# Ending a feed-forward stage on the issue of its last stores, and moving a small scale computation one step earlier

## The reference

```python
xn = _layernorm(x)
x = x + attention(xn) + ffn(xn)          # ffn: gelu, weights reduced to alpha * sign
xn = _layernorm(x)
x = x + time_mix(xn) + experts(xn)       # time_mix: a scan over time
                                         # experts: router, 2 of 8 experts, and shared ones
```

## Time and profile before

| | us |
|---|---|
| median of 3 runs | 1522.09 (1521.3 to 1522.88) |
| the profiled execution | 1525.42 |
| its span, first to last instruction | 1523.3 |
| PE / DVE / ACT / POOL busy in the span | 1321.9 / 1288.7 / 987.5 / 320.6 |
| feed-forward, start and end in the span | about 921 to 1114 |
| time-mix, start and end in the span | about 1114 to 1307 |

### The profile page before, as it was taken

One profiled execution on the slowest core, in us unless ns is written; L12 is line 12 of the kernel. 1 busy time (PEld: TensorE's weight loads), 2 busy tenths in 40 slices (PEclk: granted clock), 3 DMA queues, 4 the chain that ended last, 5 costly groups with the idle time before them and its releaser, 6 DMA issues. The chain is left out here.

```text
span 1523.3 us, 27407 instructions
## 1 busy us (share of the span) xinstructions
PE 1321.9 (87%) x9558; PEld 600.1 (39%) x9558; DVE 1288.7 (85%) x2289; ACT 987.5 (65%) x1292; POOL 320.6 (21%) x574
## 2 busy tenths in 40 slices
PE   4776999999999999999999987999667767799886
PEld 2444223232232332223233213766434334477654
DVE  6886899999999999999999914899769999755667
ACT  3452365888888888888888895666266554356541
POOL 3220000111102011020111113333000177200655
PEclk9987688999999999999999998999878879899999
DMA  6886402140424204242241025785354155776756
GB/s 207 272 262 200 63 26 45 27 85 16 82 45 67 59 6 78 45 82 45 33 88 40 11 48 160 200 279 165 140 156 144 53 174 188 230 241 208 219 174 224
DMA packets 158520, 186.15 MB, mean 122 GB/s; under 512 B 18228, under 2 KB 134708, under 8 KB 157364
## 3 DMA queue, kind: packets, MB, share of 16 engines
q1 hardware_dynamic: 135384, 151.45, 37.1%
q0 software_dynamic: 6144, 16.79, 3.4%
q10 hardware_dynamic: 16864, 16.26, 3.1%
HBM read 100.81 MB, written 83.36 MB: 121 GB/s over the span
## 5 line engine op out<-in xcount | busy, mean ns | idle before, releaser
L1324 DVE TENSOR_REDUCE att_m_part<-att_mx 128x1 f32<-128x512 f32 (+3 forms) x1152 | 680.4, 653 | 30.4 <-PE att_mx L1392 13.6
L1354 ACT ACTIVATE att_prob<-att_score,late_score_scale 128x1024 f32<-128x1024 f32 (+3 forms) x640 | 595.3, 987 | 166.1 <-PE att_score L1431 164.1
L1392 PE MATMUL att_mx<-early_kop,early_qop 48*128 48x512 f16 (+3 forms) x1280 | 354.9, 367 | 23.3 <-DVE att_neg_m L1303 6.3
L1414 PE MATMUL att_pv<-att_prob,early_v 128*32 128x512 f32 (+3 forms) x2560 | 304.1, 547 | 2.1 <-POOL att_prob L1291 2.0
L1431 PE MATMUL att_score<-early_qop,early_kop 50*128 50x512 f16 (+3 forms) x1280 | 252.9, 356 | 11.2 <-ACT att_prob L1354 10.1
L1392 PEld LDWEIGHTS att_mx<-early_kop,early_qop 48*128 48x128 f16 x1280 | 98.5, 94 | 374.3 <-DVE att_m_part L1324 346.2
L1291 POOL TENSOR_SCALAR_AFFINE_SELECT att_prob<-att_prob 128x256 f32<-128x256 f32 x256 | 103.0, 408 | 669.6 <-ACT att_prob L1354 668.8
L2193 PE MATMUL rwkv_prod<-rwkv_xm,late_mixT 128*128 128x512 f32 x192 | 99.9, 676 | 33.3 <-ACT rwkv_kvr L2147 20.2
L1431 PEld LDWEIGHTS att_score<-early_qop,early_kop 50*128 50x128 f16 x1280 | 72.1, 94 | 72.0 <-ACT att_prob L1354 56.0
L2411 POOL DMA_INDIRECT moe_yg<-results,routing_slot_i x64 | 64.1, 1002 | 133.0 <-PE moe_turn_ps L2638 102.8
L1956 POOL DMA_INDIRECT rows<-rwkv_xs,routing_slot_i x64 | 66.5, 1040 | 115.3 <-DVE routing_slot_i L2047 96.1
(11 more groups left out here) (261 smaller groups left out, 1764.6 us busy)
## 6 DMA issues: line engine op xcount, KB each, us to landing
va<-qkv_v SPq DMA_DIRECT2D x8, 1024.0 KB, 6.3
early_v<-va SPq DMA_DIRECT2D x8, 1024.0 KB, 7.3
routing_xp<-parts SPq DMA_DIRECT2D x32, 256.0 KB, 3.6
moe_xt<-rows SPq DMA_DIRECT2D x30, 256.0 KB, 3.6
rows<-att_zeros SPq DMA_DIRECT2D x8, 864.0 KB, 6.2
early_kop<-qk SPq DMA_DIRECT2D x48, 128.0 KB, 4.5
results<-moe_y ACTq DMA_DIRECT2D x24, 256.0 KB, 2.6
results<-blend_x ACTq DMA_DIRECT2D x22, 256.0 KB, 2.7
```

The lines of the kernel that those rows point to most:

```text
L1324: nc.vector.tensor_reduce(cells[:, sides[0]:sides[-1] + 1, some], mx[:, banks[0]:banks[-1] + 1, 0:len(hps) * w].rearrange("p a (h w) -> p ...
L1354: nc.scalar.activation(prob[:, r % (PROBS * HP), :, n0:], score[:, r % 2, :, n0:], ACT.Exp, scale=late_weights.score_scale[:, 0:1])\
L1392: op = nc.tensor.matmul(bank[:, n * w:(n + 1) * w], qop[rows, slot, t, hp, i * P:(i + 1) * P], kop[rows, slot, hp, c * GT:c * GT + w], sta ...
L1414: op = nc.tensor.matmul(pv[at, n0:], v[:, slot, j, at], prob[:, (st * HP + h // 2) % (PROBS * HP), h % 2, n0:], start=(j == 0), stop=(j == ...
```

## The change

Four edits.

1. The feed-forward's SP stream no longer waits for the landing of its stores. The six semaphores that count them move to `BlendInputs`, which both phases hold. The time-mix's SP stream begins with the six waits and then raises a new semaphore, `landed`. DVE waits for `landed` in the time-mix before the router's `below_top` and before the first `outcome`.
2. The two loads of the time-mix's first inputs move one round of `body` earlier on SP: they stand after `body(G - 1)` instead of after `body(G)`, five stores earlier.
3. The expert scales move ahead of the last group's low part on DVE. On PE the turn of the maxima stands ahead of the last `ln.turn` and the spread behind it.
4. The scales use a bank of `hid_ps` instead of one of `out_ps`.

```diff
@@ PowerScale
     def tensor(self, nc, pe, turn, spread, ident, ones):
+        self.tensor_turn(nc, pe, turn, ident)
+        self.tensor_spread(nc, pe, spread, ones)
...
@@ ffn_phase, SP
             for g in range(G - 2, G + 2):
                 body((g, g % 2, 0), False, g - 1 < G, True)
-                if g == G:
+                if g == G - 1:
                     sp.wait_ge(zero_stored, 16 * B)
                     sp.wait_ge(xn_out[0], 48 * (1 + T // GT // 2 + 1))
                     for b in range(B):
                         blended.load(sp, xn1T_d, b)
-            for slot in range(2):
-                sp.wait_ge(x1_out[slot], 16 * (1 + G // 2))
-                sp.wait_ge(rows_out[slot], 16 * (1 + G // 2))
-                sp.wait_ge(xn_out[slot], 48 * (1 + G // 2))
@@ ffn_phase, DVE
                 if old:
                     output(*old)
+                if older and older[0] == G - 1:
+                    expert_weights.vector(nc, dve, hid_ps[:, 0, 0:C])
+                    expert_weights.router_parts(nc, dve)
                 if older:
...
             unrolled(step, 4)
-            expert_weights.vector(nc, dve, out_ps[:, 0])
-            expert_weights.router_parts(nc, dve)
@@ ffn_phase, PE
                     if old and tile == 3:
+                        if not mid:
+                            pe.wait_ge(gelu_done.sem, gelu_done.done(G * FC - 1))
+                            expert_weights.tensor_turn(nc, pe, hid_ps[:, 0, 0:C])
                         ln.turn(nc, pe, old[0], old[1], ident[:, :])
+                        if not mid:
+                            expert_weights.tensor_spread(nc, pe, hid_ps[:, 0, 0:C])
...
             rolling(pe, step, 3)
-            pe.wait_ge(x1_done.sem, x1_done.done(G - 1))
-            expert_weights.tensor(nc, pe, out_ps[:, 0])
@@ BlendInputs
+        self.x1_out = [s.sem(f"x1_out{p}") for p in range(2)]
+        self.xn_out = [s.sem(f"xn_out{p}") for p in range(2)]
+        self.rows_out = [s.sem(f"rows_out{p}") for p in range(2)]
+        self.landed = s.sem("landed")
+
+    def wait_landed(self, eng):
+
+        for slot in range(2):
+            eng.wait_ge(self.x1_out[slot], 16 * (1 + G // 2))
+            eng.wait_ge(self.rows_out[slot], 16 * (1 + G // 2))
+            eng.wait_ge(self.xn_out[slot], 48 * (1 + G // 2))
+        eng.sem_inc(self.landed, 1)
@@ rwkv_phase, SP
+            blended.wait_landed(sp)
             for dst, src in ((consts, route_d), (count.rearrange("p two t -> p (two t)"), count_d)):
@@ rwkv_phase, DVE, below_top
+                dve.wait_ge(blended.landed, 1)
                 dve.wait_ge(const_in, 32)
@@ rwkv_phase, DVE, outcome
+                if n == 0:
+                    dve.wait_ge(blended.landed, 1)
                 nc.vector.tensor_copy(q[:, b, :, 0:1], q[:, b, :, GT:]).then_inc(q_carried, 1)
```

More of the change, by code:

```diff
@@ L151, in tensor, with tensor_turn, tensor_spread @@
     def tensor(self, nc, pe, turn, spread, ident, ones):
+        self.tensor_turn(nc, pe, turn, ident)
+        self.tensor_spread(nc, pe, spread, ones)
+    def tensor_turn(self, nc, pe, turn, ident):
         pe.wait_ge(self.found, self.first_step + 1)
         nc.tensor.matmul(turn, self.top[:, :], ident, start=True, stop=True).then_inc(self.turned, 1)
+    def tensor_spread(self, nc, pe, spread, ones):
         pe.wait_ge(self.found, self.first_step + 3)
@@ L556, in cells, with tensor_turn, tensor_spread @@
         return bank[0:n, 0:P], bank[:, P:P + n]
-    def tensor(self, nc, pe, bank):
+    def tensor_turn(self, nc, pe, bank):
+        self.scales.tensor_turn(nc, pe, self.cells(bank)[0], self.ident[:, :])
+    def tensor_spread(self, nc, pe, bank):
         pe.wait_ge(self.ones_set, 1)
-        turn, spread = self.cells(bank)
-        self.scales.tensor(nc, pe, turn, spread, self.ident[:, :], self.ones)
+        self.scales.tensor_spread(nc, pe, self.cells(bank)[1], self.ones)
     def parts_of(self, nc, dve, p, w, scale, after):
@@ L1512, in ffn_phase @@
         x1_done = s.step("x1_done", credit=2)
-        x1_out = [s.sem(f"x1_out{p}") for p in range(2)]
-        xn_out = [s.sem(f"xn_out{p}") for p in range(2)]
-        rows_out = [s.sem(f"rows_out{p}") for p in range(2)]
+        x1_out, xn_out, rows_out = blended.x1_out, blended.xn_out, blended.rows_out
         G_LOADS = 16 * (1 + KC + 1)
```

## The result

| | before | after |
|---|---|---|
| median of 8 runs, us | 1522.49 (1520.34 to 1526.49) | 1516.92 (1513.73 to 1518.38) |
| the profiled execution | 1525.42 | 1518.38 |
| its span | 1523.3 | 1516.6 |

The ratio of the times is 0.9957, with a 95% interval of 0.9944 to 0.9970. That is 4.6 to 8.5 us less, 6.5 in the middle; the medians differ by 5.6 us, the two spans by 6.7. Forecast were 6.8 us and 1515.3. The kernel is faster, by some 0.4%, and the time lies in the range.

A forecast was written before the change was run, and what follows sets the result against it. The prediction took the boundary as bound by the stores' landing, with DVE bounding the time-mix behind it. Starting at 1107.12 + 0.46 = 1107.6 instead of 1114.36 saves 6.8 us: 1522.09 - 6.8 = 1515.3, range 1512.5 to 1518.8.

The forecast's parts named there:

- The start of the time-mix: Boundary after the feed-forward: the time-mix starts at 1107.6 in place of 1114.36, 6.8 us less.
- SP last, at its own issue: End of the feed-forward: SP is the last engine through, at 1107.12, by its issue and not the landing.
- The three last issues: SP's last stores of the feed-forward: 2.8 us of issue from 1104.32, ending at 1107.12.
- 0.35 us of cover: DVE's low part, done at 1105.56, is wanted only for SP's third issue, about 1105.9, which gives the scales extra slack.
- The hand-over: From the end of SP's block to ACT's first time-mix work: 0.46 us.
- cost nil: Loads moved five stores earlier on SP: nothing is delayed; they land by 1097 and are wanted at 1107.6.
- a rival for another reason: The end of SP's block waits for the landing: start 1110.7, 3.7 us saved, 1518.4; chance 0.08 shared with a jump stall.
- The new wait: Head of the time-mix's SP stream: the last store lands at 1110.2, x of group 2 keeps 3.6 us of cover.
- the dear hand-over: Rival at SP's block end: it waits for the landing or its jump stalls, 1517.4 to 1518.8; chance 0.08.
- The rival of the late loads: Rival at the time-mix's SP head: the moved wait holds the loads, x 1.3 us late, 1516.6; chance 0.08.
- The clock: PE at the time-mix's start: 4.8 us at the low clock kept; an immediate or twice as late rise shifts 2.2 us.

The follow-up runs named there:

- e1: Changed kernel with the loads' and scales' moves taken back, only the landing wait moved: 1594.77 against 1600.23 us for the kernel before, ratio 0.9979.
- e5: Changed kernel with the expert scales put back last on DVE: 1588.93 against 1594.63 us for the kernel before, ratio 0.9970.
- e6: Changed kernel with the two loads put back where they were: 1589.96 against 1594.63 us for the kernel before, ratio 0.9979.
- e7: Changed kernel with the last low part's store issued at the head of the time-mix's SP stream: 1587.38 against 1594.63 us for the kernel before, ratio 0.9946.
- e8: The changed kernel measured again without edits: 1587.96 against 1594.63 us for the kernel before, ratio 0.9957.
- e10: Changed kernel with the last group's high and low part stored from the time-mix's SP head: 1514.87 against 1523.33 us for the kernel before, ratio 0.9945.
- e2: Kernel before with only the two loads moved five stores earlier: 1594.00 against 1600.23 us, ratio 0.9963.
- e4: Changed kernel with the landing waits kept at the feed-forward's end: 1594.46 against 1600.23 us for the kernel before, ratio 0.9972.
- e3: Kernel before with only the expert scales moved ahead of the last low part: 1598.92 against 1600.23 us, ratio 0.9991.
- e9: The kernel before profiled once more without edits, on the third chip: 1523.03 us.

## Why the prediction was right, and where not

**The start of the time-mix.** Forecast 6.8 us earlier, measured 7.15 at the boundary. SP last, at its own issue: right. ACT's first blend came at 1106.88 where 1107.6 was forecast; 0.33 of that is only that the rows were done 0.33 earlier in this profile. Two terms of the sum were off, one by 0.60 us too much and one by 0.23 too little, so 0.37 is left. The whole time can't tell 6.8 from 7.15, as both lie within its 4.6 to 8.5 us; it confirms the direction and the size, and the traces confirm the mechanism.
- The three last issues were priced at 2.8 us from 1104.32. They took from 4.13 to 6.33, 2.20 us. The issues from 1086.08 on were the wrong neighbour: the time of an issue of one and the same store varies (0.87 here, 0.98 and 1.23 in the earlier trace rows). The second issue ended at 5.35, just before the low part was ready at 5.38.
- So the "0.35 us of cover" for the scales was not there: the third issue started at 5.46, 0.08 us behind the low part, and the low part was on the path. The scales ended at 4.03, though, 0.12 ahead of the low part, so they cost nothing, as forecast.
- The hand-over was priced at 0.46 us, from a wait to the next block. From the end of a last issue it is 0.69: a drain of 0.38 us and 0.31 behind it. The drain is of the same 0.38 us in e1, e5, e6, e7, e8 and e10.

**A part I did not price.** The prediction put the loads' move at "cost nil" and used it in the next part ("With 1.05 MB of loads taken from ahead of it, the last store (issued 1105.9) lands by its median of 4.3 at 1110.2"). That sentence already held that an edit which keeps the wait would open the barrier near 1110.7 and save 3.7 us; I wrote this figure down as a rival for another reason. e2 and e4 show 4.75 us. The forecast for all edits together did not need it. A reader who takes the saving for the work of the moved wait would be wrong, though: alone it gives 5.0 us, on top of the other two 2.4.

**The new wait.** It ended at 1108.95, 9.1 us behind the rows, where I had forecast 10.0: the store landed 3.6 us after its issue, near its shortest of before (3.5), as nothing stood ahead. I had SP late for the x of group 2 by 1.8 us. It was in time: it issued at 1112.45, 5.57 us behind the start, against 5.54 before. Two things gave the 1.8 us back: the wait ended 2.1 us behind the start and not 2.6, and the four router inputs took 2.57 us of issue instead of the 3.78 that I had carried over (see the dear hand-over). Even in e1 and e6, where SP was late (18.11 and 16.76, so 8.9 and 7.8 us behind the start), ACT did not wait for group 2. The rival of the late loads falls, and by a wide margin.

**The dear hand-over.** The end of SP's block came straight behind its last issue, and nothing longer than the drain of 0.38 us stands between that issue and the barrier, in any of the six kernels that end the block so (the changed one, e1, e5, e6, e7, e10). The rival had priced 2.1 to 3.5 us, and falls; 0.23 of dearer hand-over is what there was. These traces don't record SP's branch itself, so what it took, and what the 0.38 us consist of, they don't show. That the end of a block waits for transfers in flight is ruled out too: in the changed kernel the landing came 2.1 us after the start. Yet SP does lose about a microsecond, a few issues into the new block, where it delays nobody. It shows in the kernels in which SP issues there from the start: the four router inputs take 3.78 us (before), 4.22 (e2), 3.81 (e3), 4.38 (e4) and 3.88 (e9). Where the landing wait of 1.9 us or more stands at the head, they take 2.57 each time. In e5, where that wait lasts only 0.6 us, the loss falls on the issue ahead of them:

```profile
1109.16 1.44 SPq L1934 DMA_DIRECT2D rwkv_count<-in_count  x1
```

against 0.43 in every other kernel. So 1.0 to 1.8 us are lost early in the block. Where SP stands in a wait for 1.9 us or more, no such loss shows; that the wait covers it is my reading. The rule of the Trainium skill (Runtime: NRT & Kernel Launch, section Instruction fetch mechanics) puts the stall ahead of the target's first instruction. Here none longer than the drain can stand there; a fetch of later code would fit the loss, but that is a reading and was not tested.

**The clock.** I kept the 4.8 us at the low clock and allowed 2.2 us either way. After the change the granted clock was still 0.50 from 1113 to 1114, 0.55 from 1114 to 1115 and 1.00 from then on, so it rose about 5.1 us behind the first product at 1109.79. The first 24 products took 12.96 us before and 13.08 after, and 11.97 to 13.52 over all kernels: the allowance was generous, the centre right. The tail came out 0.8 us longer (409.72 against 408.94), all of it behind the time-mix, whose length was the same to 0.01 us. In the last 23 us of the span PE's stretches at the low clock lay elsewhere; here busy time and granted clock of the changed kernel (columns as in rows 1):

```profile
1500.00:1504.00 4.00, 2.54 (x13) 1.80 (x14) 3.86 (x5) 1.24 (x2) 3.09 (x4) 0.57 0.55 163
1504.00:1508.00 4.00, 2.76 (x13) 1.66 (x11) 2.37 (x3) 0.00 (x0) 0.25 (x1) 0.57 0.38 113
```

and of the kernel before, over the same work:

```profile
1507.50:1511.50 4.00, 2.24 (x21) 2.02 (x22) 3.84 (x6) 1.24 (x2) 3.09 (x4) 1.00 0.57 189
1511.50:1515.50 4.00, 1.83 (x14) 1.26 (x12) 3.76 (x6) 0.00 (x0) 0.55 (x1) 0.90 0.43 128
```

That this is where the 0.8 us went is read from one profile of each and was not tested. The tails without a pause, 404.67 (e10), 407.3 (e9), 408.94 and 409.72, scatter by more than that; of the time-mix alone, e9 shows 191.16 us against the 192.77 of the other profile of the same kernel, so the agreement to 0.01 us is in part luck.

## What to carry to other kernels

At a phase boundary, list for every engine and every queue when it is through, and for each transfer when it lands: the start is the latest of them, and removing one wait buys only the distance to the next. Loads placed ahead of a phase's last stores in the same queue can delay the landing that the barrier waits for: here 1.05 MB of them cost 4.75 us. Look for that before you move the wait, since here it was one line and, taken alone, two thirds of the gain. Then a barrier can be shared out further: what only has to be issued can be issued on the other side of it, if a count still guards its buffer.

## What the runs showed of the hardware that I had not expected

- **A drain behind an issue.** SP's drain took 7 to 13 ns where a wait had come before it, and 379 to 381 ns where a transfer's issue had. ACT's drain behind an issue took 158 ns. None of them waits for the landing.
- **One and the same issue takes different times.** The last store of 256 KB took SP 0.87 us in the changed kernel, 0.98 in the one before, 0.80 to 1.19 in the experiments that leave it in the feed-forward, and the first issues of a block took up to 1.8 us more where SP had not stood in a wait of 1.9 us or more at its head (above).
- **A pause of 36 us.** On two chips DVE stood still in the time-mix for 36 us between two of its own instructions, in all eight profiles there (36.0 to 36.5 us), here what DVE waited for in e8 (`remote`: the profile names nothing of this core as the releaser):

```profile
DVE rwkv_y L2119 <- remote: 36.1, 1, 36.1
```

It began at 1256.5 and ended at 1292.5. POOL issued indirect transfers until 1285.44, and in all eight profiles DVE went on 6.9 to 7.5 us behind the start of POOL's last one. No profile on the third chip, and neither of the first two, shows the pause. The kernel before was not profiled on those two chips; that the pause is no part of the change is concluded from the times: on the chip of e5 to e8 the kernel before took 71.3 us more than on the third (1594.63 against 1523.33), and the changed kernel 71.0 more than in its first measurement (1587.96 against 1516.92). The pause is about half of that: in e8 the time-mix is 36.0 us longer than in the first profile of the changed kernel, and the experts' phase 32.0. The cause of either is open.
